# State scan of a selective-scan block: GpSimd multiplies two states per operation and takes 12 of 16 products with C; VectorE prepares four steps ahead

## The reference

```python
dbc = einsum('bkcl,krc->bkrl', xs, x_proj_w)      # xs: the image in 4 scan directions
dlt, b, c = (dbc[:, :, :R], dbc[:, :, R:R + N], dbc[:, :, R + N:])
dlt = softplus(einsum('bkrl,kdr->bkdl', dlt, dt_proj_w) + dt_proj_b)
dA  = dlt[..., None] * A_log
phi = exp(-cumsum(dA, axis=3))
dbx = dlt[..., None] * b * xs[..., None]
h   = phi * cumsum(dbx / (phi + 1e-12), axis=3)   # 16 states for each channel and position
y   = einsum('bkdln,bknl->bkdl', h, c) + Ds       # then the 4 directions are added
```

## Time and profile before

| | us |
|---|---|
| median of 3 runs | 3032.25 (3024.64 to 3033.62) |
| the profiled execution: its time | 3024.85 |
| its span, first to last instruction | 3023.0 |
| busy: PE, DVE, ACT, POOL | 2205.4, 2569.6, 1569.5, 1983.6 |
| granted TensorE clock, mean | 0.921 |

### The profile page before, as it was taken

One profiled execution on the slowest core, in us unless ns is written; L12 is line 12 of the kernel. 1 busy time (PEld: TensorE's weight loads), 2 busy tenths in 40 slices (PEclk: granted clock), 3 DMA queues, 4 the chain that ended last, 5 costly groups with the idle time before them and its releaser, 6 DMA issues. The chain is left out here.

```text
span 3023.0 us, 25175 instructions
## 1 busy us (share of the span) xinstructions
PE 2205.4 (73%) x7478; PEld 1083.3 (36%) x7478; DVE 2569.6 (85%) x2153; ACT 1569.5 (52%) x2283; POOL 1983.6 (66%) x1119
## 2 busy tenths in 40 slices
PE   6853666767776767777767677778986999688479
PEld 3421223333333333333333333333432555344344
DVE  5677999999999999999999999965887776789630
ACT  2565677677676767767767677743230000362220
POOL 0164999999999999999999999973000000297000
PEclk9977899999999999999999999997997999899689
DMA  1286334333343333334334343343005543100360
GB/s 47 86 240 231 99 104 119 103 121 115 104 123 104 117 114 109 119 102 123 112 110 118 104 118 104 118 142 95 0 0 153 127 112 79 38 8 8 85 86 24
DMA packets 144682, 303.92 MB, mean 101 GB/s; under 512 B 53725, under 2 KB 69220, under 8 KB 139556
## 3 DMA queue, kind: packets, MB, share of 16 engines
q1 hardware_dynamic: 143460, 298.19, 34.2%
q10 hardware_dynamic: 1088, 4.13, 0.6%
HBM read 215.46 MB, written 46.87 MB: 87 GB/s over the span
## 5 line engine op out<-in xcount | busy, mean ns | idle before, releaser
L834 POOL TENSOR_TENSOR l0c_r<-l0c_r,l0c_v 128x768 f32<-128x768 f32 x576 | 1049.2, 1843 | 25.1 <-DVE l0c_r L797 24.4
L864 ACT ACTIVATE ps<-l0c_dlt,l0c_na 128x512 f32<-128x512 f32 (+1 forms) x1152 | 625.9, 575 | 516.6 <-DVE l0c_h L823 502.7
L843 POOL TENSOR_TENSOR l0c_hcp<-l0c_cb,l0c_h 128x768 f32<-128x768 f32 x384 | 707.9, 1844 | 1.5 <-DVE l0c_h L823 1.5
L823 DVE TENSOR_TENSOR_SCAN l0c_h<-ps,l0c_h,l0c_r 128x768 f32<-128x768 f32 x384 | 693.1, 1805 | 1.2 <-issue 1.2
L755 PE MATMUL ps<-l0c_hcp,net_ident 128*128 128x512 f32 (+1 forms) x1536 | 593.4, 511 | 14.0 <-ACT l_Z L857 7.2
L874 ACT ACTIVATE l0c_r<-l0c_S,l0c_floor,l0c_na 128x768 f32<-128x768 f32 x576 | 579.7, 1013 | 0.0
L722 PE MATMUL ps<-l0c_Bp,l0c_sel 96*128 96x512 bf16 (+1 forms) x1152 | 296.7, 340 | 383.5 <-DVE l0c_hcv L804 225.0
L797 DVE SCALAR_TENSOR_TENSOR l0c_r<-l0c_r,ps 128x768 f32<-128x768 f32 x576 | 533.7, 927 | 12.8 <-PE ps L722 7.0
L755 PEld LDWEIGHTS ps<-l0c_hcp,net_ident 128*128 128x128 f32 x1536 | 274.1, 199 | 267.3 <-issue 204.6
L823 DVE TENSOR_TENSOR_SCAN l0c_h<-ps,l0c_r 128x768 f32<-128x768 f32 x192 | 335.2, 1746 | 1.0
L1429 PE MATMUL ps<-l_prod,l_wa 128*96 128x384 f32 (+1 forms) x888 | 292.3, 493 | 26.4 <-DVE l_prod L1390 26.4
(11 more groups left out here) (273 smaller groups left out, 2446.8 us busy)
## 6 DMA issues: line engine op xcount, KB each, us to landing
l0c_cb<-cf SPq DMA_DIRECT2D x768, 192.0 KB, 3.4
l_other<-l_p SPq DMA_DIRECT2D x22, 864.0 KB, 5.8
dlt<-l0s_dl SPq DMA_DIRECT2D x36, 384.0 KB, 2.3
v<-l0s_vv SPq DMA_DIRECT2D x36, 384.0 KB, 2.9
l0c_dlt<-dlt SPq DMA_DIRECT2D x36, 384.0 KB, 3.9
l0c_v<-v SPq DMA_DIRECT2D x36, 384.0 KB, 4.5
l_other<-l_p SPq DMA_DIRECT2D x22, 288.0 KB, 6.7
l0c_Bp<-bc SPq DMA_DIRECT2D x36, 144.0 KB, 4.1
```

Source lines behind the costliest of these rows:

```text
L823: dve.tensor_tensor_scan(h[:, n, :], da[j % 2], r[:, j % NR, :], init, ALU.mult, ALU.add).then_inc(s_scan, 1)
L834: pool.tensor_tensor(r[:, j % NR, :], r[:, j % NR, :], v[:, (j // N) % 2, :], ALU.mult).then_inc(s_w, 1)
L843: pool.tensor_tensor(hcp[:, p % NHP, :], cb[:, p % NCB, :], h[:, e % N, :], ALU.mult).then_inc(s_hp, 1)
L864: act.activation(da[e % 2][:, part], dlt[:, i, part], ACT.Exp, scale=na[:, i, n:n + 1]).then_inc(done, 1)
```

## The change

It touches only `l0_scan`. A product of GpSimd takes two neighbouring states at once, 128 x 2 x 768: `times_v(j)` for steps j and j + 1 (v is one operand, repeated), `times_c(e)` for two neighbouring steps of GpSimd. VectorE keeps the products with C of n = 2, 5, 10, 13; GpSimd has the pairs (0,1), (3,4), (6,7), (8,9), (11,12), (14,15). C rows come two at a time, and SP waits for the pair two back. `b_r` runs four steps ahead, r has 8 buffers, `add_y` follows five steps behind, ScalarE's decays lag six, and its store stands three steps later in the unit.

```diff
-        NR, NHV, NHP, NCB = 6, 2, 4, 4
-        AHEAD = 3
+        NR, NHV, NHP, NCB = 8, 2, 4, 4
+        AHEAD, LATE, LAG = 4, 5, 6
+        BY_VECTOR = ((2, 5, 10, 13),)
...
-        s_cb = [sem(f"cb{i}") for i in range(NCB)]
+        s_cb = [sem(f"cb{i}") for i in range(NCB // 2)]
...
+        with_c = [u * N + n for u in range(U) for n in BY_VECTOR[u % len(BY_VECTOR)]]
+        others = [j for j in range(J) if j not in with_c]
+        taken = [sum(i < j for i in with_c) for j in range(J + 1)]
+        assert all(b == a + 1 and a // N == b // N for a, b in zip(others[::2], others[1::2]))
+
         def by_pool(j):
-            return j % 3 != 0
+            return j not in with_c
 
         def dve_steps(j):
-            return (j + 2) // 3
+            return taken[j]
 
         def pool_steps(j):
-            return j - dve_steps(j)
+            return j - taken[j]
...
             for j in range(J):
                 u, n = divmod(j, N)
-                if by_pool(j):
+                if by_pool(j) and pool_steps(j) % 2 == 0:
                     t, k, c0 = place(u)
                     p = pool_steps(j)
                     if p >= NCB:
-                        sp.wait_ge(s_hp, p - NCB + 1)
+                        sp.wait_ge(s_hp, p - NCB + 2)
                     for i in range(2):
-                        sp.dma_start(cb[64 * i:64 * i + 64, p % NCB, :],
-                                     d["cf"][k, 2 * t + i, n:n + 1, c0:c0 + SEG].to_broadcast([64, SEG])
-                                     ).then_inc(s_cb[p % NCB], 16)
+                        sp.dma_start(cb[64 * i:64 * i + 64, p % NCB:p % NCB + 2, :],
+                                     d["cf"][k, 2 * t + i, n:n + 2, c0:c0 + SEG].unsqueeze(0)
+                                     .to_broadcast([64, 2, SEG])).then_inc(s_cb[p % NCB // 2], 16)
                 if n == (0 if u == 0 else 8) and u + 1 < U:
                     loads(u + 1)
...
                 if by_pool(j):
-                    pe.wait_ge(s_hp, pool_steps(j) + 1)
+                    pe.wait_ge(s_hp, pool_steps(j) // 2 * 2 + 2)
...
-            for j in range(J + 3):
+            for j in range(J + LATE):
                 if j < J and not by_pool(j):
                     c_rows(j)
                 if j + AHEAD + 1 < J:
                     b_rows(j + AHEAD + 1)
-                if j >= 3:
-                    add_y(j - 3)
+                if j >= LATE:
+                    add_y(j - LATE)
...
-                if j >= 3 * NHV:
-                    dve.wait_ge(s_y, j - 3 * NHV + 1)
+                if dve_steps(j) >= NHV:
+                    dve.wait_ge(s_y, with_c[dve_steps(j) - NHV] + 1)
...
         def _(pool):
-            for j in range(J + AHEAD + 1):
+            def times_v(j):
+                if j % N == 0:
+                    pool.wait_ge(s_in[(j // N) % 2], (j // N // 2 + 1) * (16 * NLOAD))
+                pool.wait_ge(s_ub, j + 2)
+                two = r[:, j % NR:j % NR + 2, :]
+                pool.tensor_tensor(two, two, v[:, (j // N) % 2, :].unsqueeze(1).to_broadcast([128, 2, SEG]), ALU.mult
+                                   ).then_inc(s_w, 2)
+
+            def times_c(e):
+                p = pool_steps(e)
+                pool.wait_ge(s_scan, e + 2)
+                pool.wait_ge(s_cb[p % NCB // 2], 32 * (p // NCB + 1))
+                if p >= NHP:
+                    pool.wait_ge(s_y, others[p - NHP + 1] + 1)
+                pool.tensor_tensor(hcp[:, p % NHP:p % NHP + 2, :], cb[:, p % NCB:p % NCB + 2, :],
+                                   h[:, e % N:e % N + 2, :], ALU.mult).then_inc(s_hp, 2)
+
+            for j in range(0, J + AHEAD + 2, 2):
                 if j < J:
-                    if j % N == 0:
-                        pool.wait_ge(s_in[(j // N) % 2], (j // N // 2 + 1) * (16 * NLOAD))
-                    pool.wait_ge(s_ub, j + 1)
-                    pool.tensor_tensor(r[:, j % NR, :], r[:, j % NR, :], v[:, (j // N) % 2, :], ALU.mult
-                                       ).then_inc(s_w, 1)
-                e = j - AHEAD - 1
-                if e >= 0 and by_pool(e):
-                    p = pool_steps(e)
-                    pool.wait_ge(s_scan, e + 1)
-                    pool.wait_ge(s_cb[p % NCB], 32 * (p // NCB + 1))
-                    if e >= 6:
-                        pool.wait_ge(s_y, e - 5)
-                    pool.tensor_tensor(hcp[:, p % NHP, :], cb[:, p % NCB, :], h[:, e % N, :], ALU.mult
-                                       ).then_inc(s_hp, 1)
+                    times_v(j)
+                for e in (j - 5, j - 4):
+                    if 0 <= e and e + 1 < J and by_pool(e) and pool_steps(e) % 2 == 0:
+                        times_c(e)
...
-            LAG = NR - 1
+            FIRST, LAST = LAG + LATE, N - 1
...
-                if n == LAG + 3 and 0 < u < U:
+                if n == FIRST and 0 < u < U:
                     store(u - 1)
-                late = 0 < u < U and LAG + 3 <= n < LAG + 8
+                late = 0 < u < U and FIRST <= n < LAST
...
```

More of the change, by code:

```diff
@@ L712, in _ @@
                 sp.wait_ge(s_sel[i], 16 * ((T + 1 - i) // 2))
-            for i in range(NCB):
-                sp.wait_ge(s_cb[i], 32 * pool_steps(J) // NCB)
+            for i in range(NCB // 2):
+                sp.wait_ge(s_cb[i], 32 * len(range(2 * i, pool_steps(J), NCB)))
         @block.tensor
@@ L824, in _ @@
                                        ).then_inc(s_scan, 1)
-            assert by_pool(J - 1)
+            if not by_pool(J - 1):
+                times_c(J - 1)
         @block.gpsimd
         def _(pool):
-            for j in range(J + AHEAD + 1):
-                if j < J:
-                    if j % N == 0:
-                        pool.wait_ge(s_in[(j // N) % 2], (j // N // 2 + 1) * (16 * NLOAD))
-                    pool.wait_ge(s_ub, j + 1)
-                    pool.tensor_tensor(r[:, j % NR, :], r[:, j % NR, :], v[:, (j // N) % 2, :], ALU.mult
-                                       ).then_inc(s_w, 1)
-                e = j - AHEAD - 1
-                if e >= 0 and by_pool(e):
-                    p = pool_steps(e)
-                    pool.wait_ge(s_scan, e + 1)
-                    pool.wait_ge(s_cb[p % NCB], 32 * (p // NCB + 1))
-                    if e >= 6:
-                        pool.wait_ge(s_y, e - 5)
-                    pool.tensor_tensor(hcp[:, p % NHP, :], cb[:, p % NCB, :], h[:, e % N, :], ALU.mult
-                                       ).then_inc(s_hp, 1)
+            def times_v(j):
[14 more added lines that the diff above has]
+            for j in range(0, J + AHEAD + 2, 2):
+                if j < J:
+                    times_v(j)
+                for e in (j - 5, j - 4):
+                    if 0 <= e and e + 1 < J and by_pool(e) and pool_steps(e) % 2 == 0:
+                        times_c(e)
         @block.scalar
@@ L892, in _ @@
                         decay(e + 1, own_part(e + 1), s_own)
-                if n == LAG + 3 and 0 < u < U:
+                if n == FIRST and 0 < u < U:
                     store(u - 1)
-                late = 0 < u < U and LAG + 3 <= n < LAG + 8
+                late = 0 < u < U and FIRST <= n < LAST
                 if j < J and not late:
-                    if 0 < u and n == LAG + 8:
+                    if 0 < u and n == LAST:
                         tanh(j - 1)
                     tanh(j)
-                elif late and n > LAG + 3:
+                elif late and n > FIRST:
                     tanh(j - 1)
```

## The result

| | before | after |
|---|---|---|
| median | 3027.23 us (6 runs, 3024.64 to 3033.62) | 3222.44 us (6 runs, 3215.09 to 3225.76) |
| ratio to before, 95% interval | | 1.0641 (1.063 to 1.0652) |
| the profiled execution: time, span | 3024.85, 3023.0 | 3225.76, 3223.9 |
| a unit, from the starts of the running sums | 47.44 us | 53.03 us |

The forecast was 3155 us in a range of 3070 to 3210: the right direction and, as the experiments show, the right mechanism, but a third of the loss was missing, and the range ended 12 us too low.

What follows compares the result with a forecast made beforehand. VectorE and GpSimd were taken to bound the scan together. 34 rings x (51.2 - 47.44) = 128 us, plus 2 at the start, 130 us on 3024.85, gave 3155 us; range 3070 to 3210.

Steps and rivals of the forecast that it cites:

- The mechanism: In the scan, SP's loads wait for a GpSimd product and hold VectorE's running sum, which holds GpSimd: 51.2 us a unit.
- GpSimd's pair: One GpSimd product of two states in the scan: 3.42 us (bounds 3.36 to 3.54), 14 per unit, 47.9 us.
- the ring: Per unit, running sum to v(16, 17), nine pairs to C(3, 4), loads, next sum: 51.2 us against 47.44; chance 0.76.
- rival (2): Loads land sooner and do not decide; GpSimd's own 47.9 us a unit do: 3042 us, chance 0.09.
- Rival (1): The ring holds, but a pair saves nothing, 3.54 us: ring 52.3 us, total 3193 us, chance 0.10.
- rival (3): VectorE's 46.0 us a unit decide, given a GpSimd pair of at most 3.29 us: 2978 us, chance 0.05.
- The marks: Profile signs: VectorE idle about 5 us before nearly every running sum, GpSimd idle 2 to 3 us before v(16, 17).
- from that end to landed loads: From the end of C(3, 4) through SP's issues to the next unit's landed loads: 9.2 us, bounds 7.4 to 10.7.
- VectorE's leg and the handovers: VectorE from the running sum's start in step 10 to L797 for step 17, 11.05 us; two handovers, 0.2 us.
- the top corner: Both upper extremes at once, pair 3.54 and loads 10.7 us: ring 53.8 us, total 3243 us, left out as unlikely.

Runs made afterwards that it cites:

- the first experiment: The changed kernel with the next unit's five loads issued after the C rows of step 6, not step 8: 3031.91 us, ratio 1.0023.
- the second experiment: The changed kernel with the five loads issued ahead of the C rows of steps 8 and 9, release unchanged: 3105.18 us, ratio 1.0261.
- the single-product kernel: The kernel of the first experiment with each two-state GpSimd operation split into two of one state: 3104.49 us, ratio 1.0261.

## Why the prediction was right and where it was wrong

**The mechanism holds.** Moving the loads by one place in SP's order takes the loss away; moving them in the kernel before brings one about; shortening the stretch from release to sum in two ways shortens the unit by about what it takes out. The other parts that were costed at nothing were nothing: four steps ahead (1.0004), TensorE's and ScalarE's new distances (in the first experiment, which has them too, GpSimd is full), and the supply of C rows, though they land after 5.5 us where I had priced them by 3.4 and 3.9.

**GpSimd's pair** was forecast at 3.42 us and takes 3.400; without the ring the unit is 47.51 us, forecast 47.9. The estimate from the Trainium skill's GPSIMD Engine Reference, § 3.1, 3.38 us, was as near; the page measured its 4497 ns on an addition, where the prediction says product, and what it sets against the shared read port is loop overhead, not dispatch. That GpSimd becomes the longer engine once the ring is open, rival (2), is what the first experiment shows, at 3031.9 us against the 3042 given; it did not come about in the changed kernel. Rival (1) falls with the 0.14 us that a pair saves, rival (3) with GpSimd full at 3.40 us, where it asked for 3.29.

**The marks** named beforehand are there: idle time before nearly every running sum (230 us in all, forecast some 170), ended by Cp's landing; GpSimd's idle time before v(16, 17), 2.31 us; starts of the sums 53 us apart (forecast 51). One was missed: v(14, 15) waits too, 2.24 us.

**The step that failed is the term "from that end to landed loads"**, 9.2 us with an upper bound of 10.7. In the turn shown the stretch up to the sum is 10.06; by the medians of landing and the issues of that turn the term is 0.03 + 1.27 + 2.15 + 7.3 = 10.75, above my bound. I had put the doubled C rows in front of the loads at 0.5 us, because a 384 KB load (dlt) had landed 0.5 us later than 192 KB of C rows. But C rows of 384 KB land 2.1 us later than those of 192 KB (5.5 against 3.4), and Cp behind them goes from 5.5 to 7.3, which the second experiment undoes (5.6). Size was the wrong likeness: dlt was priced where nothing of double size ran ahead of it. Of the 1.55 us by which the term is too small, 1.3 are the landing, and 0.2 are slower issues (1.27 for the pair against 1.13, 2.15 against 2.05).

The doubled rows ahead are not the whole of the 1.8 us, though. In the first experiment Cp is issued behind the same rows and lands after 6.4 us (6.3 in the single-product kernel, whose queue has the same order). What differs there, by the timelines, is that the next C rows leave 6.9 us after Cp, which by then has landed as a rule; in the changed kernel they leave 3.5 us after it (both medians), while it is under way. No run moves these rows alone, so how the 1.8 us divide between what runs ahead and what follows stays open.

**VectorE's leg and the handovers** were 11.05 + 0.2, and take 11.47 from the running sum's start to v(16, 17) in the turn shown (1043.61 - 1032.14), to which the end of C(3, 4) adds 0.04: 0.3 more. With nine pairs, 30.6: 10.75 + 11.47 + 30.6 + 0.04 = 52.9, against 53.03 measured and 51.2 forecast. By the means of the 34 units, 10.88 + 11.52 + 30.64, the first stretch is 1.7 over its forecast, the second 0.3 over, the third 0.2 under. 34 units make 62 us of the difference.

**The rest.** Of the 201 us between the two profiled executions 34 x 5.59 = 190 are the ring. The first running sum of the loop starts 6.2 us later (343.3 against 337.1), where 2 were forecast, and the stretch from the last sum to the end is 4.8 us longer, forecast as nothing. The first experiment, with the same order at the start of the scan, has its sum at 337.3, so most of the 6 us is no property of the change; 5.0 of them are there before the very first running sum, which starts at 304.2 us against 299.2. At the end, the last scan ends 63.5 us after the last running sum and ended 65.4 after it before the change, so the 4.8 us arise behind the scan, in code that the change leaves alone.

**The range** erred by taking the largest landing seen, 7.0, plus 0.5 as the outer bound, and then by cutting the top corner as unlikely. A ring's bound must allow for what the change does to each resource on it, and the DMA queue was the one where the change doubled the data just ahead of the loads. The total is also closer than the failed term alone would put it, since a pair was priced 0.02 us too long, nine times in the ring.

## What to carry to other kernels

When a kernel's order is written out by hand, look at what stands **behind** a moved wait on the same queue: here the change moved a wait for C rows from the product of step 2 to the pair of steps 3 and 4, and five loads that had nothing to do with it then held VectorE for 6.8 us, once per unit. Write the ring out (who releases the load, who waits for it, and how that one comes back to the releaser) and compare its length with the work of the fullest engine. When two engines are both full, moving work pays only up to the point where they are level again: here pairs saved 73 us, the 48 products more that GpSimd was given took all of it back, and returning one pair in every third unit made the gain.

## What the runs showed of the hardware

How soon a load lands depends on its neighbours in the queue. Cp is 144 KB in every kernel here. By the medians it lands 5.5 us after its issue where the C rows ahead of the five loads are 2 x 192 KB, and 5.6 where they are 2 x 384 KB but follow the loads. Where 2 x 384 KB go ahead, it takes 7.3 in the changed kernel and 6.4 in the first experiment.

GpSimd's recorded durations can't be priced with: in the single-product experiment a 768-element product is recorded at 2202 ns, in the kernel before at 1843, and in both its starts lie 1.77 us apart. The page of the single-product kernel has this row, and in its timeline ten products pass between the starts at 998.21 and 1015.90 us, 1.769 each:

```profile
L842 POOL TENSOR_TENSOR l0c_r<-l0c_r,l0c_v 128x768 f32<-128x768 f32 x576 | 1113.3, 2202 | 19.6 <-DVE l0c_r L803 19.6
```

TensorE's granted clock falls with the stalls. Between 900 and 1200 us it is 0.91 on average in the changed kernel (1 is 2.4 GHz), where TensorE waits for VectorE's L803 up to 10 us at a time, 0.97 before and 0.98 in the first experiment. In the turn shown it is 1.00 from 1020 to 1025 us; TensorE then stands 8.52 us, with 0.81 granted from 1025 to 1032 us and 0.62 from 1032 to 1042 (means of stretches in which part is at the lower level, 1.2 GHz), and from 1042 to 1055 it is 1.00 again. Two matmuls of B rows take 0.84 us in that slow stretch and 0.50 outside it. Whether this is part of the 0.3 us of VectorE's leg was not tried.
